# A two-layer graph network: the order of DVE's and ACT's operations within a step of the first layer

## What is computed

```
enc   = cos((node_vec[src] - edge_weight)[:, None] * time_w + time_b)      # 32 columns
e     = concat([enc, edge_attr_64]) @ We                                   # 96 -> 128
q, k, v = x @ Wq + bq, x @ Wk + bk, x @ Wv + bv
alpha = sum(q[dst] * (k[src] + e)) / 8            # one for each edge and head
a     = softmax of alpha over the edges of one dst
out   = segment_sum((v[src] + e) * a, dst) + x @ Wskip + bskip
x     = layernorm(x + out)
x     = layernorm(x + segment_sum(edge_weight * x[src], dst) @ W1.T + b1)
```

## Time and profile before

| | |
|---|---|
| time, median of 3 runs | 9850.37 us (9843.33 to 9854.15) |
| the profiled execution | 9864.48 us |
| span of its instructions | 9862.8 us |
| busy over the span | PE 77%, weight loads 72%, DVE 87%, ACT 52%, POOL 68% |
| mean granted clock of PE | 0.822 |

### The profile page before, as it was taken

The page is one execution under the profiler, slowest core; times in us unless marked ns, Lnnn a source line. Parts: engine busy times, 40 slices in busy tenths (PEclk is TensorE's granted clock), DMA queues, the critical chain, the costliest instruction groups (busy, mean ns, idle before and its releaser), DMA issues.

```text
span 9862.8 us, 272152 instructions
## 1 busy us (share of the span) xinstructions
PE 7624.6 (77%) x52868; PEld 7101.3 (72%) x52869; DVE 8560.3 (87%) x21301; ACT 5115.0 (52%) x20838; POOL 6708.6 (68%) x6871
## 2 busy tenths in 40 slices
PE   6477777777777777777756777788888888888855
PEld 2477777777777777777756777787888877877754
DVE  5899999999999999999987666799999999999968
ACT  2377777777777777777753333333333333333300
POOL 0477777777777777777745777777777777777720
PEclk8688988888888888898875555688888888888888
DMA  6467666676666666666632222355555555555544
GB/s 191 114 180 178 179 177 177 178 179 178 176 177 180 177 176 177 178 181 177 177 97 69 71 71 71 106 151 147 149 147 149 148 148 149 148 148 149 148 133 116
DMA packets 1631706, 1484.67 MB, mean 151 GB/s; under 512 B 792007, under 2 KB 1363043, under 8 KB 1631203
## 3 DMA queue, kind: packets, MB, share of 16 engines
q1 hardware_dynamic: 1374244, 848.34, 34.3%
q0 software_dynamic: 257088, 632.95, 22.8%
HBM read 1225.51 MB, written 254.87 MB: 150 GB/s over the span
## 4 chain that ended last, share of the span: by engine, by line
issue 25%; DVE 19%; POOL 18%; PE 14%; DMA 7%; ACT 7%; DVEq 6%; SPq 3%; ACTq 2%; POOLq 0%
POOL message_scratch L869 17%; DMA message_scratch<-ohT,idx 6%; PE bank L982 3%; DVE y_all L1537 3%; PE bank L973 3%; ACT arena L1154 2%; DVEq L531 2%; PE bank L955 2%; PE bank L1015 2%; PE bank L963 2%; DVE acc L1670 1%; SPq L728 1%; DVE oh L1583 1%; DVE oh L1576 1%; DVE kve L1523 1%
## 5 line engine op out<-in xcount | busy, mean ns | idle before, releaser
L817 POOL DMA_INDIRECT kv<-kv_scratch,arena x3136 | 3265.7, 1041 | 1236.6 <-issue 837.5
L869 POOL DMA_INDIRECT message_scratch<-ohT,idx x3232 | 3214.2, 994 | 1079.0 <-issue 880.2
L1261 ACT ACTIVATE ohT<-bank,kv 128x128 f32<-128x128 f32 x3232 | 923.9, 369 | 2703.8 <-DMA message_scratch<-ohT,idx 2665.1
L1154 ACT ACTIVATE arena<-arena,weights 128x65 f32<-128x65 f32 x7040 | 1771.6, 337 | 2.4 <-PE bank L982 2.3
L1063 PE MATMUL bank<-acc,oh 128*128 x6464 | 1211.2, 345 | 520.3 <-ACT ohT L1262 514.4
L1063 PEld LDWEIGHTS bank<-acc,oh 128*128 128x128 f32 x6464 | 1054.7, 247 | 627.7 <-issue 625.2
L1077 PE MATMUL bank<-oh,kve 128*128 128x128 f32 x8640 | 1387.7, 321 | 144.7 <-DVE arena L1838 107.8
L982 PE MATMUL bank<-arena,oh 128*128 128x130 f32 x7040 | 1164.1, 318 | 280.8 <-DVE acc L1670 274.8
L1077 PEld LDWEIGHTS bank<-oh,kve 128*128 128x128 f32 x8640 | 1248.0, 227 | 167.8 <-issue 157.3
L982 PEld LDWEIGHTS bank<-arena,oh 128*128 128x128 f32 x7040 | 1048.2, 227 | 362.6 <-issue 295.1
L973 PE MATMUL bank<-arena,ohT 128*128 128x128 f32 x7040 | 1090.6, 306 | 0.0
(11 more groups left out here) (232 smaller groups left out, 12653.6 us busy)
## 6 DMA issues: line engine op xcount, KB each, us to landing
kve<-message_scratch SPq DMA_DIRECT2D x2160, 129.0 KB
kve<-nodes_scratch SPq DMA_DIRECT2D x880, 256.0 KB
feat<-in_edge_attr_dram SPq DMA_DIRECT2D x880, 96.0 KB
feat<-block_scratch SPq DMA_DIRECT2D x812, 98.0 KB
arena<-q_scratch SPq DMA_DIRECT2D x880, 64.0 KB
message_scratch<-ohT,idx POOLq DMA_INDIRECT x3232
kv<-kv_scratch,arena POOLq DMA_INDIRECT x3136
feat<-in_edge_attr_dram SPq DMA_DIRECT2D x880, 32.0 KB
```

What stands on the lines that cost most here:

```text
L817: pool.indirect_dma_start(kv[:, k, g, :], None, kv_d, bass.IndirectOffsetOnAxis(ap=group_rows[:, half, k * G + g, 0:1].bitcast(I32), axis= ...
L869: pool.indirect_dma_start(msg_d, bass.IndirectOffsetOnAxis(ap=idx[:, k, g:g + 1], axis=0), sum_ring[:, k % RING1, g, :], None).then_inc(s_ ...
L1154: op = act.activation(wv[:, st.k % 2, g, h, :], vR[:, st.k, g, h, :], ACT.Copy, scale=weights[:, st.k // ROUND, g, st.k % ROUND, h:h + 1])
L1261: act.activation(sum_ring[:, st.k % RING1, g, 0:C], banks[2 + st.k % 2][:, g * P:(g + 1) * P], ACT.Copy, scale=taken[:, st.k, g, 2:3])
```

## The change

It changes the order of stages in two turns' lists of the first layer, and nothing that is computed.

- DVE: onehot_stage, which stood after product_stage and the first two stages of the running maximum, becomes the first of the turn. ve_stage and ke_stage follow. The three angle operations, which stood first, after ve_stage and after ke_stage, now stand after ke_stage, after onehotT_stage and after product_stage.
- ACT: arg_stage, which was after the sine for the step 18 ahead, becomes the first stage of the turn, for the step 17 ahead. The turns in which ACT loads its group numbers move with it.

```
--- before.py
+++ after.py
@@ -1166,7 +1166,7 @@
                 enc = encodings(st)
                 act.activation(enc, enc, ACT.Sin, bias=zero[:, :], scale=-2.0 * PI_BELOW).then_inc(s_enc, 1)
 
-            EDGES, group1 = {0: 6, 6: 8, 14: 2}, {}
+            EDGES, group1 = {0: 7, 7: 8, 15: 1}, {}
 
             def arg_stage(st):
 
@@ -1210,12 +1210,12 @@
             def body(i):
                 for k in range(UNROLL0):
                     if k in EDGES:
-                        groups_stage(mybir.EngineType.Activation, group1, Step(i, k + 18), EDGES[k])
+                        groups_stage(mybir.EngineType.Activation, group1, Step(i, k + 17), EDGES[k])
                     sines = [(sine_stage, 16)] if k % BATCH == 0 else []
                     gaps = [(gap_stage, 7)] if first_of(k, 7, ROUND) else []
                     smalls = [(smallc_stage, 5)] if first_of(k, 5, ROUND) else []
                     exps = [(exp_stage, 3), (dropx_stage, 3)] if first_of(k, 3, ROUND) else []
-                    at(i, k, (featc_stage, 15), (weigh_stage, 2), *sines, (arg_stage, 18), *gaps, *exps, *smalls)
+                    at(i, k, (arg_stage, 17), (featc_stage, 15), (weigh_stage, 2), *sines, *gaps, *exps, *smalls)
 
             act.wait_ge(s_const2, 1)
             act.wait_ge(s_load, 16 * N_LOADS)
@@ -1686,9 +1686,9 @@
                     def once(ahead, *stages):
                         return [(stage_of, ahead) for stage_of in stages] if first_of(k, ahead, ROUND) else []
 
-                    at(i, k, *turn[0], (ve_stage, 14), *turn[1], (ke_stage, 14), *turn[2], (block_stage, 0), *once(5, forward_stage),
-                       (onehotT_stage, 15), *once(5, backward_stage), (product_stage, 13), *once(4, run_stage, first_stage),
-                       (onehot_stage, 2), *once(11, rel0_stage), *once(4, col_stage, drop_stage), (alpha_stage, 13), *once(4, new_stage), *once(3, shift_stage),
+                    at(i, k, (onehot_stage, 2), (ve_stage, 14), (ke_stage, 14), *turn[0], (block_stage, 0), *once(5, forward_stage),
+                       (onehotT_stage, 15), *turn[1], *once(5, backward_stage), (product_stage, 13), *turn[2], *once(4, run_stage, first_stage),
+                       *once(11, rel0_stage), *once(4, col_stage, drop_stage), (alpha_stage, 13), *once(4, new_stage), *once(3, shift_stage),
                        (sum_stage, 0), *once(8, pen_stage), *once(2, keep_part(0), keep_part(1), keep_part(2)))
 
             pipeline(dve, body)
```

## The result

The changed kernel takes 9898.0 us, the median of 4 runs (9893.2 to 9901.03). The kernel before took 9851.22 us in the 4 runs beside it (9843.33 to 9854.15). The ratio is 1.0048, with a 95% interval of 1.0033 to 1.0063: slower by 47 us, where 9840 us was forecast and 9895 us was the upper end of the range. The profiled execution took 9901.03 us, with a span of 9899.3 us against 9862.8 us before, 36.5 us more. (The profiled execution before, 9864.48 us, was some 14 us above the median of its kernel, so the two profiles show 10 us less of a difference than the medians.)

The account below looks back on a forecast made before the run. A round was taken as an ACT and PE chain plus DVE's own work. Terms -0.08, -0.26 and +0.25 gave -0.09 us a round, -10 us over 110 rounds: 9840 us; own range 9831 to 9869, eight in ten 9785 to 9895.

Parts of the forecast that it names:

- The two pieces of a round: Eight turns, T0 to T7: ACT and PE chain, new_stage to T0's ve_stage (16.5 us), then DVE's work to new_stage (24.7).
- (a) to (c): T6, T7 and T0 up to ve_stage: DVE arrives 0.56 us sooner, mostly waiting longer for PE; net -0.08 us a round.
- (d): T0 behind ve_stage: onehot's 0.60 us leaves, an angle operation's 0.34 comes, with the round waiting for DVE: -0.26 us.
- (e): T4: the onehot no longer covers semaphore waits and the scan's end before col_stage; cost 0 to 0.60, taken as +0.25 us.
- S: Follow-up theory: alpha directly behind product waits 0.1 us and holds DVE's sequencer, delaying T2's register load: 0.4 us a round.
- (b)'s reason: T7: ve_stage's issue idle would hide under a onehot of 0.60 us: -0.3 us, between 0 and -0.43.
- (f) and ACT: Later third angle operations and sines in T0, T2, T4 cost nothing; ACT's reordered products in T6, 0.6 us cover, cost nothing.
- rival 3: ACT's products behind exp come too late in T6, L1503 still waiting for L1178: slower, 9862 to 9906 us, chance 0.06.
- Rival 1: DVE decides the round after all: faster, 9813 us, or 9784 to 9746 if last in T0 too; chance 0.36.
- Rival 2: PE falls to its lower clock in T1 after about 1.0 us idle: 9887 us in half the rounds; chance 0.13.
- Rival 4: DVE's order costs issue time elsewhere, T4's cost at its full 0.60 us: +0.26 us a round, 9879 us; chance 0.03.
- (c): T0 up to ve_stage: earlier savings mostly become longer waiting for PE; -0.08 us, between 0 and -0.56 (own range: -0.2).

Follow-up runs that it names:

- products off the chain: Kernel before, with ACT's arg_stage (18 ahead) at the head of odd turns and behind the sine in even ones: 9806.92 us, ratio 0.9952.
- Onehot behind alpha: Kernel before, with the onehot moved from ahead of alpha_stage to behind it in T1, T3 and T7 only: 9902.89 us, ratio 1.0053.
- ACT's part alone: Kernel before, DVE untouched, with ACT's changed list and register loads: 10,057.55 us, ratio 1.0211.
- late angles alone: Changed kernel with the onehot back in its old place in every turn, angle operations late, ACT new: 9946.69 us, ratio 1.0086.
- kernel with both edits: Kernel before, onehot and onehotT ahead of ve_stage in even turns, later angle operations moved, ACT's arg_stage at odd heads, behind even sines: 9667.76 us, 0.9812.

## Why the prediction was wrong, point by point

**The two pieces of a round** held: chain and DVE's piece add up to the round in every kernel of the table, and "products off the chain" moved one of them alone.

**(a) to (c), T6, T7 and T0 up to ve_stage**: -0.08 us forecast, +0.02 measured. As said, DVE's savings there only made the wait for PE longer: idle before ve_stage rose to 2.03 us in a round (2.5 was named), and T0's ve_stage did not come sooner.

**(d) T0 behind ve_stage**: -0.26 forecast, -0.39 measured.

**(e) T4**: +0.25 forecast, +0.07 measured up to new_stage. The profile shows no idle time before any of the small operations; "a few tenths before L1619" was named.

**The step that failed** is the one ahead of them, "I cost each place by what it does to the two pieces of the round": places were costed in T6, T7, T0 and T4, and T1, T2 and T3, in the middle of DVE's piece, were left at nothing. The onehot was there too, between product and alpha, and (e) had asked of T4 what it covers and not of the odd turns. In even turns an angle operation took its place; in T1, T3 and T7 nothing did. The missing term measures +0.13 (T1), +0.27 (T2) and +0.23 (T3), +0.63 us in a round. With it the sum is +0.02 - 0.39 + 0.07 + 0.63 = +0.33 us, and by 110 rounds 36 us, the 36.5 us of the spans. All four are measured, so this says where the time is, not why; of the 47 us between the medians it leaves 10, which is within the spread of one execution. The two terms that were right in sign gave 0.32 back, so the loss is the difference of two larger numbers.

That what stands between product and alpha in the odd turns is the cause is shown three ways: putting the onehot back there takes the ratio from 1.0048 to 0.9924, putting the block sums there instead, with the onehot still first, takes it to 0.9995, and making the adjacency alone in the kernel before costs as much (1.0053). The 0.63 us have two main parts. The first is alpha's later start, 0.10 us in T1 and 0.15 in T3, 0.25 together. It is the wait for the product's end; alpha both reads the product and waits for its semaphore, and no run separates the two.

The second is the register load of T2, whose turn grew by 0.27 us. S had the waiting alpha hold up DVE's sequencer, so that the load starts late: it starts 0.52 us before the end of T1's block sums in the changed kernel and 1.00 us before the end in the kernel before. But measured from T1's product it isn't late at all. It starts 1.25 us after the product's start in both kernels, and takes 0.84 us (1.06 in the body's other round). In both, the register work queued behind alpha begins 0.05 us after the product's end. What changed is the cover: with the onehot gone from T1 its last operation ends 1.77 us after the product's start instead of 2.25, so that the load ends 0.31 to 0.55 us behind the turn's end instead of -0.16 to +0.07, and DVE stands still for 0.42 to 0.67 us. "Onehot behind alpha" agrees: there the load starts 1.03 us before the end of T1, where S named 0.5, and T2 isn't longer, since a whole onehot lies behind alpha and covers it. The loads of DVE in the changed kernel (least/median/largest ns, 1000 to 4500 us; the least is that at the body's start):

```profile
L517 DVEq TENSOR_LOAD <-walk_rows x122: 750/836/1079, 1013.4 to 4493.9; - x122
```

So S was right that the two go together, and wrong on how. The remaining 0.11 us, in T1 and T3, were not traced.

**(b)'s reason** was that a first onehot hides register work. It did at T7, which went from 4.86 to 4.65 us, and idle before L1518 for issue fell from 35.4 to 1.3 us. It failed where loads stand in front of the onehot itself: "idle before L1559 small" came out as 1.10 us in a round. The work isn't hidden by being first, but by what ran before it.

**(f) and ACT.** L1503's idle fell to 0.24 us in a round (below 0.3 was named). The cover in T6 was put at 0.6 us and measures 0.55 in the round shown (2027.37 to 2027.92). It isn't always there: the whole 0.24 us is a wait for L1178 in T6, in 30 of 81 rounds, up to 1.0 us, and that was the sign named for rival 3. It cost nothing that shows, for with ACT's list of before the wait is gone and the time the same (1.0045 against 1.0048).

**Rival 1** did not come: DVE's own piece became longer. **Rival 2** named 9887 us, the nearest number, but it isn't what happened: the idle time of PE before T1 grew to 0.94 us, as worked out (1.0), and the passes behind it ran at the upper level; the clock is 0.89, and ve_stage of T2 doesn't wait for PE in any round. After 2.12 us (before L955 at 2031.64) the next eight passes took 1.90 us. The Trainium skill ("TensorE: Matmul & The Clock Gate", section "HAM oscillation — how this bites in real kernels") has idle gaps of PE bring the clock down, with longer ones than these in its example; here the gap of 2.12 us was followed by the lower level and that of 0.94 us was not. **Rival 4** put the cost of DVE's order in T4, with 0.03 of the chance; the kind of cost was right, its place and turns were not.

**Table loads.** The next activation starts 0.02 us behind the load at 2024.68, and the products were in time. The drain of about 1.38 us that the Trainium skill ("ScalarE: Activation LUTs", section "What ACT_TABLE_LOAD costs") adds isn't there in this kernel, and weighing the row above the page was right.

**The range.** The forecast's own range, 9831 to 9869 us, doesn't follow from the terms given for it: with (e) between 0.05 and 0.45 and (c) between 0 and -0.2 the sum runs from -0.41 to +0.19 us in a round, 9805 to 9871 us. That doesn't touch the result; no such pair of values reaches 9898 us.

**Open.** Putting the onehot back in odd turns also made the chain 0.30 us shorter, which neither part explains, and gained more than the loss. ACT's part alone and late angles alone cost more than worked out: their waits are shown, their exact sums aren't. The kernel with both edits on the slow chip is 0.45% slower, on the usual one 1.9% faster; the cause of that chip's time wasn't found.

## What to carry to other kernels

Before moving an instruction, list in every turn which pair it separates, and cost the new neighbours, not only the old and the new place: a reduction directly behind the product that it reads waits, and a register load queued behind the pair has less work left to hide under. If a filler is needed elsewhere, leave another in its place, and put fillers in front of the instruction that waits for another engine. Then look at the chain itself: taking ACT's products off it was worth 0.5% alone, and with the 1.6% of DVE's reordering it made 1.9%.

## What the runs showed of the hardware

- A DVE instruction of 128x512 that reads the result of the one directly ahead, and waits for its semaphore, starts 0.70 us after it instead of 0.60 (T1 of the changed kernel). One small operation fits in between at no cost (rel0_stage in T5, alpha 0.72 us behind product). Three such places in a round cost 0.5% of the kernel ("onehot behind alpha").
- A register load of 0.84 to 1.06 us at the head of a turn showed as 0.42 to 0.67 us of "issue" idle time, and one at the start of the loop's body (0.75 us) as 1.08 us, depending on how much work was queued ahead of it. "Issue" idle time can be removed by a change elsewhere: putting the onehot back in T1 took that of T2 from 0.55 to 0.09 us.
- In the round shown of the changed kernel PE was at its upper level after 0.94 us without work (eight passes in 1.13 us), and at its lower one after 2.12 us (1.90 us).
- One chip ran the kernel before in 13,124 us. From 1000 to 4500 us (windows view and a group of "onehot behind alpha" there) DVE's instructions take as long as elsewhere, 682 ns, but there are 500 ve_stages in place of 649, the granted clock is 0.79, and the waits are long and have no releaser within the core:

```profile
1000.00:4500.00 3500.00, 2489.45 (x15374) 2298.86 (x15373) 2478.76 (x5719) 2019.59 (x7122) 1880.20 (x2053) 0.79 0.53 136
```

```profile
L1518 DVE TENSOR_TENSOR arena<-kv,bank 128x512 f32<-128x512 f32 x500 | 341.1, 682 | 682.5 <-remote 600.6 <-PE bank L963 56.0 <-issue 24.4
```
